# Fewer and longer products of zeros in a recurrence, block states on four tiles of the array, and products of zeros among transposes

## The reference

```python
# 1. a recurrence over 512 steps, 8 sequences at once
xw = x @ Wx + b
h = tanh(xw[t] + h @ Wh)            # 256 x 256, h goes from step to step
# 2. a convolution of each channel in time with its own kernel (a diagonal state space layer)
K[m, l] = sum_n C_re[m, n] * exp(dt[m] * A[n] * l)
x = x + causal_conv(u, K) + u * D    # u: the states of layer 1
# 3. a gated linear recurrence with sigmoid gates, then a mixture of 16 experts (2 a token) with a shared expert
x = x + shared_mlp(hidden) + experts(hidden)
```

## Time and profile before

| | us |
|---|---|
| median of 3 runs | 973.94 (973.1 to 974.42) |
| the profiled execution, its own time | 974.19 |
| its span, first to last instruction | 972.3 |
| PE busy / PEld busy | 924.3 / 777.5 |
| ACT busy / DVE busy / POOL busy | 506.3 / 410.7 / 299.1 |

### The profile page before, as it was taken

One profiled execution on the slowest core, in us unless ns is written; L12 is line 12 of the kernel. 1 busy time (PEld: TensorE's weight loads), 2 busy tenths in 40 slices (PEclk: granted clock), 3 DMA queues, 4 the chain that ended last, 5 costly groups with the idle time before them and its releaser, 6 DMA issues.

```text
span 972.3 us, 64880 instructions
## 1 busy us (share of the span) xinstructions
PE 924.3 (95%) x28864; PEld 777.5 (80%) x28864; DVE 410.7 (42%) x781; ACT 506.3 (52%) x1735; POOL 299.1 (31%) x324
## 2 busy tenths in 40 slices
PE   7999999999999999999999998999899999999993
PEld 5888888888888888996444446788899999999993
DVE  1000010100001103553899799875564646556450
ACT  2444444444444446443876587134465656566551
POOL 3111111111111110650003463760045364554545
PEclk6799999999999999999999999999999999999997
DMA  2222222221111111111001110533357666675634
GB/s 89 83 92 87 95 93 87 100 85 33 35 40 36 35 33 28 66 76 57 0 1 39 49 56 22 184 116 108 127 132 162 133 157 119 151 146 127 134 40 53
DMA packets 69161, 80.34 MB, mean 83 GB/s; under 512 B 24225, under 2 KB 53558, under 8 KB 69122
## 3 DMA queue, kind: packets, MB, share of 16 engines
q1 hardware_dynamic: 54242, 62.18, 20.3%
q0 software_dynamic: 14592, 17.10, 10.7%
q10 hardware_dynamic: 288, 0.56, 0.2%
HBM read 44.16 MB, written 33.83 MB: 80 GB/s over the span
## 4 chain that ended last, share of the span: by engine, by line
PE 81%; issue 5%; ACT 4%; POOL 4%; DVE 3%; DMA 2%; POOLq 0%; SPq 0%; ACTq 0%; DVEq 0%
PE ps L516 19%; PE ps L811 16%; PE ps L508 9%; PE ps L825 8%; PE ps L677 8%; PE ps L489 6%; PE ps L727 3%; POOL slots_in L447 2%; PE ps L577 2%; ACT tok L879 2%; PE ps L590 2%; PE ps L736 2%; PE ps L599 2%; PE ps L494 2%; DMA slots_in<-tok,arena 1%
## 5 line engine op out<-in xcount | busy, mean ns | idle before, releaser
L516 PE MATMUL ps<-tok,wh 128*32 128x8 f32 x16384 | 255.2, 180 | 12.9 <-issue 3.5
L879 ACT ACTIVATE tok<-ps 128x8 f32<-128x8 f32 x1024 | 155.9, 177 | 204.0 <-PE ps L516 201.6
L516 PEld LDWEIGHTS ps<-tok,wh 128*32 128x32 f32 x16384 | 220.0, 113 | 48.0 <-ACT tok L879 25.2
L466 POOL DMA_INDIRECT out<-arena,dest x80 | 127.9, 1599 | 99.3 <-ACT arena L1030 76.9
L489 PE MATMUL ps<-zero 128*32 128x192 bf16 x1920 | 141.1, 255 | 0.0
L418 POOL TENSOR_TENSOR big<-tok,zero 128x128 f32 x64 | 29.0, 453 | 322.0 <-ACT tok L879 322.0
L811 PE MATMUL ps<-xgT_hi,ew_hi 128*128 128x320 f32 (+1 forms) x384 | 119.5, 311 | 3.2 <-DVE spare L1275 1.6
L811 PE MATMUL ps<-xgT_hi,ew_lo 128*128 128x320 f32 (+1 forms) x384 | 119.5, 311 | 0.0
L811 PE MATMUL ps<-xgT_lo,ew_hi 128*128 128x320 f32 (+1 forms) x384 | 119.0, 310 | 0.0
L1143 DVE TENSOR_TENSOR arena<-arena,pack 128x256 f32 x32 | 13.6, 426 | 246.3 <-ACT arena L884 246.3
L1381 DVE TENSOR_TENSOR mid<-mid,ps 128x320 f32<-128x320 f32 (+1 forms) x96 | 46.6, 486 | 107.0 <-ACT mid L1048 57.5
(11 more groups left out here) (206 smaller groups left out, 1643.5 us busy)
## 6 DMA issues: line engine op xcount, KB each, us to landing
slots_in<-mid SPq DMA_DIRECT2D x16, 645.0 KB, 3.7
mid<-slots_in SPq DMA_DIRECT2D x16, 645.0 KB, 4.2
arena<-in_ex_down SPq DMA_DIRECT2D x16, 384.0 KB
arena<-in_ex_gate SPq DMA_DIRECT2D x16, 352.0 KB
arena<-in_ex_up SPq DMA_DIRECT2D x16, 352.0 KB
xst<-in_x_steps SPq DMA_DIRECT2D x66, 64.0 KB, 1.8
xtok<-in_x_tok SPq DMA_DIRECT2D x16, 256.0 KB, 2.7
mid<-k_pad SPq DMA_DIRECT2D x32, 128.0 KB, 3.1
```

Source lines behind the costliest of these rows:

```text
L466: pool.indirect_dma_start(out=out[:, :], out_offset=bass.IndirectOffsetOnAxis(ap=dest[:, z, t:t + 1], axis=0), in_=yo[:, z, t], in_offset= ...
L516: last = nc.tensor.matmul(sums_at(bank, t, o)[Q * j:Q * j + Q], wh[:, k, columns(j, o)], hring[:, (n - 1) % (2 * G), k], start=False, stop ...
L879: nc.scalar.activation(hring[:, n, o], sums_at(n // G, n % G, o), ACT.Tanh).then_inc(s_h[o], 1)
```

## The change

In the recurrence the 192 columns of zeros behind 15 of 16 steps become 320 columns behind seven of them (n = 0, 2, 4, 6, 10, 12, 14). Steps 1, 3, 5, 9, 11, 13 keep only their input's share, step 15 has nothing behind it. The eight instructions of `kernel_sums` are split: four behind step 7, four behind step 8. A wait on `s_ps0`, long fulfilled, is dropped. Among the transposes each group from the second on is followed by one product of zeros, 128 x 128 weights and 256 bf16 columns, into bank 0. In the convolution the states of odd channels are written to the other half (`h = k ^ c % 2`), so `block_states` uses all four tiles; even channels' states lie at the end of one bank, odd ones' at the start of the next (banks 0 and 1 or 6 and 7). `carried` is split by even and odd channels: own block, wait for the scan of this chunk, even half, states of the next chunk, wait for the even half (`s_half`), odd half. `stand` writes into the chunk's own bank. The constants that belong to odd channels are crossed on the host, one more block of 128 columns (`dt_s`) is loaded and gets its own exponential, and DVE clears two more banks' first columns after the first group of transposes.

```diff
@@ -68,9 +68,9 @@
-        sizes = (C * B, NST, 1, P + KP, P, IT, KP * C * KP, 8, HB, RB, R + CT)
+        sizes = (C * B, NST, 1, P + KP, P, P, IT, KP * C * KP, 8, HB, RB, R + CT)
-        h0r, a_bc, a_q, dt_q, c_q, d_k, masks, consts, iota_t, resets_t, rows_to = [pack[:, sum(sizes[:n]):sum(sizes[:n + 1])] for n in range(len(sizes))]
+        h0r, a_bc, a_q, dt_q, dt_s, c_q, d_k, masks, consts, iota_t, resets_t, rows_to = [pack[:, sum(sizes[:n]):sum(sizes[:n + 1])] for n in range(len(sizes))]
@@ -238,6 +239,15 @@
+        psf = ps[:, :, :].rearrange("p n t -> p (n t)")
+
+        def states_at(z):
+
+            return psf[:, 512 * 6 * z + 256:512 * 6 * z + 768]
+
+        def place_of(c):
+
+            return CP // 2 * (c % 2) + c // 2
@@ -390,19 +400,19 @@
-                pool.tensor_tensor(pw[:, m % 2], dt_q[:, CP * m:CP * m + CP].unsqueeze(2).to_broadcast([P, CP, NST]),
+                pool.tensor_tensor(pw[:, m % 2], dt_s[:, CP * m:CP * m + CP].unsqueeze(2).to_broadcast([P, CP, NST]),
-            pool.wait_ge(s_dtm, 3)
+            pool.wait_ge(s_dtm, 4)
-                pool.tensor_tensor(d0[:, m % 2], lam[:, CP * m:CP * m + CP].unsqueeze(2).to_broadcast([P, CP, RB]),
-                                   resets_t.unsqueeze(1).to_broadcast([P, CP, RB]), ALU.mult).then_inc(s_d0, 1)
+                pool.tensor_tensor(d0[:, m % 2].rearrange("p (e c) r -> p e c r", e=2), lam[:, CP * m:CP * m + CP].rearrange("p (c e) -> p e c", e=2).unsqueeze(3).to_broadcast([P, 2, CP // 2, RB]),
+                                   resets_t.unsqueeze(1).unsqueeze(1).to_broadcast([P, 2, CP // 2, RB]), ALU.mult).then_inc(s_d0, 1)
@@ -488,11 +498,12 @@
                 for j in range(J):
                     nc.tensor.matmul(ps[Q * j:Q * j + Q, 6, 0:columns], zero16[:, 0:Q], zero16[:, 0:columns], start=True, stop=True, tile_position=(0, Q * j))
 
-            def kernel_sums():
-
-                for c in range(KP):
+            def kernel_sums(half):
+
+                for c in range(KP // 2 * half, KP // 2 * half + KP // 2):
                     last = nc.tensor.matmul(ps[0:C * KP, 4, 0:HB], cblk[:, c], kq[:, c], start=c == 0, stop=c == KP - 1, skip_group_check=True, tile_position=(0, 0))
-                last.then_inc(s_kmm, 1)
+                if half == 1:
+                    last.then_inc(s_kmm, 1)
 
             def inputs_summed(bank, n):
 
@@ -541,13 +552,14 @@
                         last = inputs_summed(1 - bank, u)
                         if u == NIN - 1:
                             last.then_inc(s_xdone, 1)
-                    if n != G - 1:
-                        keep_groups_up(192)
+                    if n in (0, 2, 4, 6, 10, 12, 14):
+                        keep_groups_up(320)
                     if n == G - 1:
-                        pe.wait_ge(s_ps0, 1)
                         pe.wait_ge(s_kqe, i + 1)
                         pe.wait_ge(s_kc, i + 1)
-                        kernel_sums()
+                        kernel_sums(0)
+                    if n == G:
+                        kernel_sums(1)
             pe.wait_ge(s_state, 16)
             with pe.Fori(0, IT) as i:
                 for bank in range(2):
@@ -564,6 +576,10 @@
                 for b in range(4):
                     last = nc.tensor.transpose(ps[:, 2 + n % 4, b * P:(b + 1) * P], uT[:, tb].rearrange("p k t b -> p (k t) b")[:, :, 4 * bq + b], ident[:])
                 last.then_inc(s_utr, 1)
+                if n == 1:
+                    pe.wait_ge(s_xc, 1)
+                if n >= 1:
+                    nc.tensor.matmul(ps[:, 0, 0:256], zero16[:, 0:P], zero16[:, 0:256], start=True, stop=True)
 
             def rows_of_half(k):
 
@@ -573,9 +589,10 @@
 
                 for c in range(CP):
                     for k in range(C):
-                        to = ps[rows_of_half(k), z, RB * c:RB * c + RB].rearrange("p (b t) -> p b t", t=NB)[:, :, 1:NB]
+                        h, at = k ^ c % 2, RB * place_of(c)
+                        to = states_at(z)[rows_of_half(h), at:at + RB].rearrange("p (b t) -> p b t", t=NB)[:, :, 1:NB]
                         last = nc.tensor.matmul(to, pw[rows_of_half(k), z, c], u_tok[rows_of_half(k), CP * z + c].rearrange("p (b t) -> p b t", t=NB)[:, :, 0:NB - 1],
-                                                start=True, stop=True, skip_group_check=True, tile_position=(HB * k, HB * k))
+                                                start=True, stop=True, skip_group_check=True, tile_position=(HB * k, HB * h))
                 last.then_inc(s_tmm, 1)
 
             def to_tokens(z, c, k, odd):
@@ -591,17 +608,19 @@
                                                     start=c == 0, stop=False, skip_group_check=True, tile_position=(HB * k, HB * odd))
                 last.then_inc(s_own, 1)
 
-            def carried(z):
-
-                for c in range(CP):
-                    for k in range(C):
+            def carried(z, crossed):
+
+                for c in range(crossed, CP, 2):
+                    for h in range(C):
                         for odd in range(2):
-                            last = nc.tensor.matmul(to_tokens(z, c, k, odd), qd[rows_of_half(k), CP * z + c], xc[rows_of_half(k), z, c].rearrange("p (r e) -> p r e", e=2)[:, :, odd],
-                                                    start=False, stop=True, skip_group_check=True, tile_position=(HB * k, HB * odd))
-                last.then_inc(s_qmm, 1)
-            def stand():
-
-                nc.tensor.matmul(ps[0:Q, 6, 0:B], zero16[:, 0:Q], zero16[:, 0:B], start=True, stop=True, tile_position=(0, 0))
+                            last = nc.tensor.matmul(to_tokens(z, c, h ^ crossed, odd), qd[rows_of_half(h), CP * z + c], xc[rows_of_half(h), z, place_of(c)].rearrange("p (r e) -> p r e", e=2)[:, :, odd],
+                                                    start=False, stop=True, skip_group_check=True, tile_position=(HB * h, HB * odd))
+                last.then_inc((s_half, s_qmm)[crossed], 1)
+
+            def stand(z):
+
+                at = R * CP
+                nc.tensor.matmul(ps[0:Q, 2 + 2 * z, at:at + B], zero16[:, 0:Q], zero16[:, 0:B], start=False, stop=False, skip_group_check=True, tile_position=(0, 0))
             pe.wait_ge(s_uev, NB)
             pe.wait_ge(s_uea, SLOTS)
             pe.wait_ge(s_xc, 1)
@@ -614,17 +633,17 @@
                     m = 2 * i + z
                     pe.wait_ge(s_x1, m + 1)
                     pe.wait_ge(s_slot_tz[z], 16 * i + 16)
-                    stand()
+                    stand(z)
                     own_block(z)
+                    pe.wait_ge(s_xc, m + 2)
                     pe.wait_ge(s_pe, m + 2)
-                    pe.wait_ge(s_xc, m + 1)
                     pe.wait_ge(s_uea, 2 * m + SLOTS - 1)
-                    stand()
+                    stand(z)
+                    carried(z, 0)
                     block_states(1 - z)
-                    pe.wait_ge(s_xc, m + 2)
-                    pe.wait_ge(s_uea, 2 * m + SLOTS - 2)
-                    stand()
-                    carried(z)
+                    pe.wait_ge(s_half, m + 1)
+                    stand(z)
+                    carried(z, 1)
 
             def x1_turned(b):
                 for c in range(C):
@@ -867,6 +886,7 @@
+            nc.scalar.activation(dt_s[:], dt_s[:], ACT.Exp).then_inc(s_dtm, 1)
@@ -1156,7 +1176,9 @@
-            nc.vector.memset(ps[:, 0:2].rearrange("p n (c t) -> p (n c) t", t=NB)[:, :, 0], 0.0).then_inc(s_xc, 1)
+            nc.vector.memset(ps[:, 0:2].rearrange("p n (c t) -> p (n c) t", t=NB)[:, :, 0], 0.0)
+            dve.wait_ge(s_utr, 1)
+            nc.vector.memset(ps[:, 6:8].rearrange("p n (c t) -> p (n c) t", t=NB)[:, :, 0], 0.0).then_inc(s_xc, 1)
@@ -1166,7 +1188,7 @@
-                nc.vector.tensor_tensor_scan(xc[:, z].rearrange("p c r -> p (c r)"), d0[:, z].rearrange("p c r -> p (c r)"), ps[:, z, :], 0.0, ALU.mult, ALU.add).then_inc(s_xc, 1)
+                nc.vector.tensor_tensor_scan(xc[:, z].rearrange("p c r -> p (c r)"), d0[:, z].rearrange("p c r -> p (c r)"), states_at(z), 0.0, ALU.mult, ALU.add).then_inc(s_xc, 1)
@@ -1444,8 +1466,13 @@
-    masks[:, np.arange(KP), :, np.arange(KP)] = (half[:, None] == np.arange(C))[None]
+    masks[:, np.arange(KP), :, np.arange(KP)] = (half ^ np.arange(KP)[:, None] % 2)[:, :, None] == np.arange(C)
+
+    def crossed(v):
+        w = v.reshape(C, P, -1).copy()
+        w[:, 1::2] = w[::-1, 1::2]
+        return w
...
```

More of the change, by code:

```diff
@@ L232, in build @@
         s_own = sem("s_own")
+        s_half = sem("s_half")
         s_slot_tz = [sem("s_slot_tz0"), sem("s_slot_tz1")]
@@ L1457 @@
     tri = np.stack([np.triu(np.ones((P, P)), 1) - 1, np.ones((P, P))], 1).astype(f32)
-    pack = (rows(cond.T), np.broadcast_to(a_log, (P, NST)), np.tile(a_log, C), np.concatenate([np.repeat(dt.reshape(C, P), HB, 0), over], 1),
-            c_re.reshape(C, P, NST).transpose(0, 2, 1), d_k, masks, consts, np.broadcast_to(-np.arange(HB, dtype=f32), (P, HB)),
```

(2 more changed lines are left out.)

## The result

The kernel after takes **990.37 us** (989.31 to 992.79, 4 runs) against 974.18 for the kernel before on the same chip: ratio **1.0157, 95% [1.0111, 1.0202]**. It is slower than before, 35.6 us above the forecast of 954.8, and outside the range. The kernel before takes 1010.7 to 1015.4 us in 7 of its 53 executions over all comparisons, and executions set off so from the rest are left out of a ratio.

The account below looks back on a forecast made before the run. PE was taken as the bound: a ring of products and tanh in the recurrence, PE outright in the blocks. 11.6 + 0.4 - 1.7 + 9.0 - 0.2 = 19.1 us off gave 954.8 us, range 948 to 966.

Parts of the forecast that it names:

- The step that failed: Blocks: PE bounds them outright, busy 58.35 of 59.70 us at a granted clock of 1.00, and is again the bound after.
- its rival in the recurrence: Recurrence: with fewer zeros the clock falls again and again; 1008 us if half the turns run at half clock; chance 0.12.
- Recurrence: Recurrence: bare steps behind biases save 0.22 us a turn, split kernel sums 0.16; 11.6 us over 30.5 turns.
- The jump's 0.07: Recurrence, loop's jump: step 15 loses its zeros; taken at nothing, gain bounded by 0.07 us a turn, 2.1 us.
- The zeros of 320 columns: Recurrence: longer zeros fit behind their steps; taken at nothing, loss bounded by 0.04 us at two places a turn, 2.4 us.
- one fall more of 27 us: Rival: the clock falls one time more, 30 steps at half clock cost 6.6 us, 961 us; chance 0.06.
- Transposes: Transposes: 15 more products of zeros find no hole; 14 cost 1.7 us, bounds nothing and 3.4.
- States on four tiles: Blocks: 32 state instructions on four tiles take 0.53 us instead of 1.06; 17 times, 9.0 us saved.
- Splitting `carried`: Blocks: adds no instruction, stands stay three a chunk, and the new wait on `s_half` costs nothing.
- The old pace: Rival, blocks: states stay at two tiles' pace, by the bank or the moving operands; 964 us, chance 0.07.
- First wait for the scan: Blocks, first chunk only: own block follows the first states, so PE waits for the scan; 0.2 us lost.

Follow-up runs that it names:

- e10_after_shifted: The changed kernel with 24 warm-up products of 170 columns instead of 8 of 512: 958.83 us once, 983.02 to 987.15 in the other five.
- e5_full_zeros: The changed kernel with one full-array product of zeros ahead of each stand, 48 more: 1002.69, 971.07, 1003.09 and 1005.58 us.
- e9_rec_aligned: The kernel before with the recurrence's part of the change alone and 38 warm-up products of 108 columns instead of 8 of 512: 960.22 us, ratio 0.9855.
- e8_before_full_zeros: The kernel before with one full-array product of zeros ahead of each stand, 48 more: 988.2, 988.41, 991.15, 985.88 us, ratio 1.0112.

## Why the prediction was wrong

**The step that failed** is the sentence that put the blocks' clock down as given: "58.35 of 59.70 us busy" at 1.00, "in the blocks PE is the bound outright". I asked of the clock only in the recurrence and the transposes, where the change takes zeros away or adds them, and priced its rival in the recurrence (1008 us at 0.12). It fell where nothing was taken from PE's work: 83.0 us of blocks where 3.08 us a chunk at full clock would make 16 x 3.08 + 0.7 = 50, and 3.4 more in the gates. That makes 36 us, with a microsecond or two of stalls in it. Executions of one kernel with and without the fall are 24 to 28 us apart in e10_after_shifted (958.8 against 983.0 to 987.2) and 32 to 35 in e5_full_zeros.

The profile held the warning: in the earlier trace rows the clock falls behind stretches in which PE pauses (it fell a third time, at 960.08 us, where the prediction counts two), and before's timeline has a stall in its blocks that I didn't look for, since 0.45 us are small as time.

**The terms themselves:**
- *Recurrence*, 11.6 forecast. A turn is 10.80 us (15 steps of 0.67 to 0.68 and one of 0.71) against 11.26 before: 0.46 saved in place of 0.38, which makes 14.0 over 30.5 turns. The jump's 0.07, taken at nothing and kept as a bound, came about. The stage gave 11.2 in the profile of after, since its first half-clock stretch ran to 46.9 us instead of 35.1; e9_rec_aligned and e10_after_shifted, with stretches to 35.4 and 32.3, give 15.5 and 16.3. The zeros of 320 columns held no step up.
- *The clock in the recurrence*: 1.00 over 319.9 us. The rival as I placed it didn't come, and one fall more of 27 us neither.
- *Transposes*: 1.26 us to the first states, 1.7 forecast. The Trainium skill ("TensorE: Matmul & The Clock Gate", Part 4) says that a transpose doesn't count as PE-busy in the same way as other products. No profile shows a fall during them, with or without the products.
- *States on four tiles*, 9.0 forecast. They take 0.60 us and not 0.53; that is the missing size. Splitting `carried` cost next to nothing, as forecast: 64 products in one go take 1.07 us, two halves 0.48 and 0.60. The first chunk of e10_after_shifted, the one at full clock and without a stall, is 3.41 us (373.86 to 377.27) less 0.33 of waiting for the scan, so 3.08 against 3.53: 0.45 x 16 + 0.4 = 7.6 us. The old pace, a rival, is out. The Trainium skill ("TensorEngine Tiling (Array Packing)", Gotcha 1) says that different row tiles can't access one PSUM bank at the same time. It didn't bring the old pace back: both row halves write each bank of the states here, and the 32 products take 0.60 us. No row shows two of them at the same moment.
- *First wait for the scan*, 0.2 forecast: 0.33 in e10_after_shifted, in the first chunk only. As time it was rightly sized.

By these the sum is 14.0 - 1.3 + 7.6 - 0.3 = 20.0 us, near the 19.1 forecast, but by terms read one by one: recurrence 2.4 more than forecast, states 1.4 less. No whole execution shows it. The one of e10_after_shifted without a fall is 15.4 us below before's 974.2, and e9_rec_aligned, with before's states, is already at 960.2. So the recurrence's gain is shown in whole executions, and the states' gain only in the pieces of a timeline. The clock outweighed them all.

## What to carry to other kernels

Ask of every stage, and not of those alone that an edit touches, what its first microseconds look like at the granted clock: here a fall cost 24 to 38 us, more than any term of the change, and 15 short products 380 us earlier could make it common. Judge the parts of a change in executions in which the clock holds, and give a kernel near the edge several executions before one is believed. Where a stage of small tiles runs through its code for the first time, count PE's products to its stalls and try moving the code. Or lay full-array work there, if it costs less than the fall.

## What the runs showed of the hardware

- On 64 x 64 float32 tiles the clock, once down, stayed at 0.50 for 81.9 to 99.0 us though PE was busy 86.6 of 88.7 us (after). In all nine profiles that have the fall it came back 6.7 to 9.5 us after the blocks' end, in the gates' products of the full array. In before's recurrence, at its start, it took 27.3 us.
- Stalls of 0.4 to 1.3 us, start to start, at places 126 products apart (each with its weight load), in code that runs for the first time. They ended 1.27 to 1.55 us after a 16,384-byte packet of the instruction queue had landed.
- A single product of the full array between groups of small tiles took 0.21 us of PE's time (e8_before_full_zeros), against 0.12 among its like the earlier trace rows.
